# An adaLN layer with routed experts: late blocks every 11 steps, the count a step later, the w2 wait at its first reader

## What is computed

```python
mod = (_silu(L0_c) @ L0_wmod).reshape(L0_c.shape[0], 6, 1, -1)
sa, ca, ga, sb, cb, gb = (mod[:, 0], ..., mod[:, 5])
ga = (2 * (ga >= 0) - 1) * jnp.maximum(jnp.abs(ga), 0.25)   # gb likewise
h = _layernorm(x, axis=-1) * (1 + ca) + sa
x = x + ga * _L0_attn_ref(h, L0_attn_W_qkv, L0_attn_W_o)    # causal, 16 heads of 16
h = _layernorm(x, axis=-1) * (1 + cb) + sb
x = x + gb * _L0_ffn_ref(h, L0_ffn_router_w, L0_ffn_w1, L0_ffn_w2)
```

## Time and profile before

| | us |
|---|---|
| runs | 2679.83, 2695.54, 2696.79 |
| median | 2695.54 |
| profiled execution | 2677.67 (span 2676.0) |
| experts, from 2124 us to the end | 552 |
| TensorE busy, share of the span | 93% |
| VectorE, ScalarE, GpSimd | 80%, 65%, 21% |

### The profile page before, as it was taken

How to read it: one execution, slowest core, us unless ns; L and a number is a source line. 1 busy time by engine, 2 the same in 40 slices (tenths; PEclk the granted TensorE clock), 3 DMA queues, 4 the chain that set the end, 5 groups by cost and what they waited for, 6 DMA issues and landing times. The chain is left out here.

```text
span 2676.0 us, 51675 instructions
## 1 busy us (share of the span) xinstructions
PE 2484.6 (93%) x16164; PEld 1259.0 (47%) x16164; DVE 2138.3 (80%) x5454; ACT 1727.2 (65%) x3555; POOL 563.3 (21%) x496
## 2 busy tenths in 40 slices
PE   7988999999999999999999999999999699989996
PEld 6863333333333333333333333333332288889896
DVE  6989989888888988888888888888882287867775
ACT  4650576677766666666666666666667566657775
POOL 3451000000001011010101101010101145665554
PEclk9996899999999999999999999999999899999998
DMA  5873224525536363544626353554524556766643
GB/s 193 275 249 89 75 92 149 178 105 157 160 107 191 112 181 110 175 142 147 189 97 191 124 167 117 172 161 139 175 102 156 185 139 152 180 174 133 109 104 70
DMA packets 268011, 396.35 MB, mean 148 GB/s; under 512 B 61712, under 2 KB 163344, under 8 KB 267504
## 3 DMA queue, kind: packets, MB, share of 16 engines
q1 hardware_dynamic: 145504, 164.08, 21.2%
q10 hardware_dynamic: 80240, 151.56, 16.0%
q0 software_dynamic: 42016, 77.59, 12.7%
HBM read 141.16 MB, written 253.00 MB: 147 GB/s over the span
## 5 line engine op out<-in xcount | busy, mean ns | idle before, releaser
L1078 ACT ACTIVATE probs<-ps 128x512 f32<-128x512 f32 (+3 forms) x2400 | 1121.7, 538 | 553.4 <-PE ps L1388 329.8
L1100 DVE TENSOR_REDUCE early<-ps 128x1 f32<-128x512 f32 x1536 | 1000.3, 684 | 111.5 <-PE ps L1293 106.2
L1293 PE MATMUL ps<-kh,qs 96*128 96x512 bf16 (+3 forms) x2560 | 881.9, 362 | 75.4 <-DVE early L1100 34.1
L1388 PE MATMUL ps<-qs,kh 99*128 99x512 bf16 (+3 forms) x2560 | 829.3, 351 | 17.4 <-ACT probs L1078 7.1
L1404 PE MATMUL ps<-probs,vs 128*17 128x512 f32 (+3 forms) x5120 | 598.5, 539 | 0.0
L1293 PEld LDWEIGHTS ps<-kh,qs 96*128 96x128 bf16 x2560 | 250.9, 99 | 688.3 <-DVE early L1100 299.4
L1096 DVE CUSTOM_DVE_ANT_0 junk<-ps,causal 128x128 bf16<-128x128 f32 (+3 forms) x1024 | 480.1, 483 | 49.7 <-PE ps L1293 45.8
L1388 PEld LDWEIGHTS ps<-qs,kh 99*128 99x128 bf16 x2560 | 245.5, 98 | 294.1 <-ACT probs L1078 130.9
L1646 POOL DMA_INDIRECT out<-y,to x142 | 240.4, 1693 | 218.0 <-DVE y L1838 80.1
L982 POOL DMA_INDIRECT rows_out<-row,place_a x96 | 93.4, 973 | 692.0 <-DVE place_a L777 604.9
L1392 PE MATMUL ps<-ident_b,causal_b 128*128 128x128 bf16 x1024 | 213.8, 220 | 0.0
(11 more groups left out here) (246 smaller groups left out, 2866.9 us busy)
## 6 DMA issues: line engine op xcount, KB each, us to landing
rows_out<-empty ACTq DMA_DIRECT2D x129, 1056.0 KB, 4.8
contexts<-ctx_out SPq DMA_DIRECT2D x64, 256.0 KB
xg<-rows_out SPq DMA_DIRECT2D x25, 544.0 KB
q_parts<-parts SPq DMA_DIRECT2D x32, 384.0 KB, 3.4
k_parts<-parts SPq DMA_DIRECT2D x32, 384.0 KB, 4.5
qs<-q_parts SPq DMA_DIRECT2D x64, 192.0 KB, 7.5
kh<-k_parts SPq DMA_DIRECT2D x64, 192.0 KB, 9.0
v_ones<-vt SPq DMA_DIRECT2D x16, 544.0 KB, 5.2
```

The source lines that it names most:

```text
L1078: nc.scalar.activation(probs[u % PB][:, h, q0:TB], bank(s % SB)[:, q0:TB], ACT.Exp, scale=SCALE).then_inc(exp_done, 1)
L1100: nc.vector.tensor_reduce(early[:, h, t, k0 // CW:k0 // CW + 1], tile, AX.X, ALU.max).then_inc(max_done, 1)
L1293: nc.tensor.matmul(tile[:, 0:w], qh[a % HR][0:STACK, t * P:(t + 1) * P], kh[a % HR][0:STACK, k0:k0 + w], start=True, stop=True).then_inc(m ...
L1388: mm = nc.tensor.matmul(tile[:, q0:TB], kh[a % HR][:, kt * P:(kt + 1) * P], qh[a % HR][:, j * TB + q0:(j + 1) * TB], start=True, stop=not ...
```

## The change

Three constants and one wait are changed. PITCH goes from 12 to 11, so the blocks begin at steps 1, 12, 23 and 34. L_COUNT and L_PUT go from 18, 19 to 19, 20. What is computed from them moves: LATE_TABLE 58 to 56; SEND_FROM (4, 7, 10, 12) to (4, 7, 10, 11); STORE_AT (7, 10, 13, 16) to (7, 9, 12, 15); FETCH_X_AT (7, 10) to (7, 9); FETCH_AT stays (0, 4, 7, 10). On GpSimd the token numbers of block 3's rows are written behind add(9), not add(10). TensorE's wait for the split of w2 moves from ahead of the loop into step 1, behind up(3) and ahead of down(0).

```diff
-PITCH = 12
+PITCH = 11
 BASE = [1 + PITCH * m for m in range(LATE_BLOCKS)]
...
-L_ROUTE, L_EXP, L_COMPARE, L_ORDER, L_SHARE, L_COUNT, L_PUT = 14, 15, 16, 17, 17, 18, 19
+L_ROUTE, L_EXP, L_COMPARE, L_ORDER, L_SHARE, L_COUNT, L_PUT = 14, 15, 16, 17, 17, 19, 20
...
                 up(0)
                 up(1)
-                pe.wait_ge(w2l_done, SPLITS // 2)
-                pe.wait_ge(w2lp_done, SPLITS - SPLITS // 2)
                 for q in range(NQ):
...
                     if q + 2 < NQ:
                         up(q + 2)
+                    if q == 1:
+                        pe.wait_ge(w2l_done, SPLITS // 2)
+                        pe.wait_ge(w2lp_done, SPLITS - SPLITS // 2)
                     if q:
                         down(q - 1)
```

## The result

The changed kernel takes 2699.5 us (median of 10 runs, 2694.0 to 2707.4), the kernel before 2685.2 us (median of 10 runs, 2679.8 to 2696.8). The ratio is 1.0045, with a 95% interval of 1.0028 to 1.0063: slower by 0.45%, 12 us. Forecast was 11 us faster. The three runs of before that were shown first happened to hold the two highest of the ten (and the lowest), so their median, from which the forecast was counted, lies 10 us above that of all ten; from 2685.2 us the same 11 us lead to 2674.

What follows compares the result with a forecast made beforehand. TensorE was taken to set the experts' pace until the last 21 half tiles' adds, then GpSimd's scatter-adds. Gains of 2.9, 7.9 and 2.7 us less 2.6 gave 11 us off 2695.5: 2684.5 us, range 2663 to 2699.

Steps and rivals of the forecast that it cites:

- the counts: TensorE's four waits ahead of the counts, 8.9 us: running each count a step later wins 7.9 us (bounds 5 and 8.9).
- so no new wait is seen: Count, put and their users move a step; TensorE's down(BASE + 22) already waits for VectorE's next step, so no added wait.
- the sum: Whole change: 13.5 us earlier at step 56, less 2.6 us at the last block's sends, so 11 us less.
- The prediction's own sign of being wrong: Forecast wrong if new hid_lo waits exceed 5 us before step 56, or the gap ahead of tile 15 is absent.
- 2.9: Start of the experts: gain in us from moving the w2 wait, with up(4) held by VectorE's low_rows(1); bounds 2 and 5.8.
- Part 1: The wait for the split w2: down(0) comes 3.4 us earlier, of which 2.9 us is taken as gain.
- The counts and their clock: Ahead of step 56: 7.9 us from count waits, 2.7 us from slow clock behind the second and third (bounds 0 and 2.7).
- hidden: Tile 17's gather lands at T(56) + 33.2, its transposes are due at T(56) + 35.8: covered by 2.6 us.
- The last sends: Block 3's sends ahead of add(12): down(60) waits until T(56) + 26.7 us; the stretch grows by 2.6 us (bounds 0.9 and 5.4).
- the same lengths as now: From 2413 us to the end, the changed kernel's lengths were to match those of the kernel before.
- The prediction's premise: In the last 21 half tiles GpSimd's scatter-adds pace the work, starting on VectorE's gated sums; earlier gains reach the end.
- The slower one: Rival, chance 0.06: late placement delays the last block's sends, add(12), weigh(14) and tile 17's gather; 2700 us at 15 us late.

Runs made afterwards that it cites:

- after_sends4: The changed kernel with blocks 0 and 1 sending four rows' DMAs behind each add instead of three: 2683.5 us, ratio to before 0.9993.
- after_project3: The changed kernel with the first half of a late block's projection at step 3 of the block instead of 2: 2692.0 us, ratio to before 1.0029.
- pitch_only: The kernel before with only PITCH 11, counts and w2 wait at their old places: 2702.1 us, ratio to before 1.0061.
- count_only: The kernel before with only L_COUNT and L_PUT one step later, at pitch 12: 2675.7 us, ratio to before 0.9969.
- w2_only: The kernel before with only the wait for the split w2 moved to its first reader: 2684.6 us, ratio to before 0.9999.
- w2_dve: The kernel before with the w2 wait in step 1 and all w2 low parts made on VectorE: 2674.3 us, ratio to before 0.9966.
- after_sends12: The changed kernel with SEND_FROM[3] back at 12, so add(12) precedes block 3's eight sends: 2696.0 us, ratio to before 1.0042.
- after_two: The changed kernel with blocks 0 and 1 sending four behind each add and block 3's sends behind add(12): 2684.5 us, ratio to before 1.0014.
- after_three: The changed kernel with four sends per add, block 3's sends behind add(12) and the projection's first half a step later: 2668.6 us, ratio to before 0.9948.
- after_four: The kernel of after_three with all low parts of w2 made on VectorE: 2666.2 us, ratio to before 0.9949.
- after_pitch12: The changed kernel with PITCH back at 12: 2673.7 us, ratio to before 0.9954.

## Why the prediction was wrong, point by point

**The step that failed** stands under the counts: "so no new wait is seen", and in the sum, where the pitch itself had no term. I looked for what becomes later or is queued behind something. A shorter pitch makes a late block's parts earlier against everything that isn't tied to the pitch: the adds and sends, which go by tiles. I gave the pitch a row for put and the next transposes and for SyncE's loads, and none for the three other waits between blocks. The prediction's own sign of being wrong, new waits for hid_lo of over 5 us before step 56, came with 15.7 us (4.9, 4.0 and 6.8). The three waits were all in the code that I had read:

- centre(m) waits for the sends of block m - 2. SEND_FROM of blocks 0 and 1 stays 4 and 7, so the last sends stand behind add(6) and add(9), which start in VectorE's steps 31 and 43. Centre came in steps 35 and 47, four behind; it comes in steps 33 and 44, two and one behind. At block 1, four adds, two sends and the landing take about 12 us (2331.25 to 2343.1), three to four steps. This is 14 to 16 us of the loss, shown by after_sends4.
- project(m + 1, 0) waits for turned(m). It moved from the step in which route(m) already waits for the same thing to the step ahead of it: 5.4 us in three waits, gone in after_project3.
- late_transposes(m) waits for modulate(m), a step further on VectorE. At pitch 12 every block falls on the same phase of a tile (BASE is 1 modulo 4); at pitch 11 the phase goes round, onto steps where w1_low or gate_sums can stand ahead of modulate: 6.0 us in three waits. But pitch_only, with the same phases, has 1.3 us of them and count_only, at pitch 12, 3.7. So the larger part comes with the count's new step and not with the phase; that TensorE is then earlier, because it no longer waits for chosen_r, is my reading and no run shows it by itself.

**The w2 wait.** Down(0) came 3.2 us earlier, with 3.4 predicted, and for the reason given. The step from there to "2.9" was wrong: it took the two ups at 1.2 GHz, so that they would fill the pause, and they ran at full clock, so that a gap of 4.9 us was left. In w2_only TensorE's clock behind it was low until about 2160, where before it had risen by 2157. With the granted clock at 0.58 from 2152 to 2160, 2.3 of the 3.2 us were given back by T(16). Part 1 counted a slow clock inside the pause and none behind the new gap. The Trainium skill (SBUF — State Buffer, "Who interferes with whom") has the two engines exclude each other there. The runs agree: in w2_dve, where GpSimd has nothing to do at that place, the 4.44 us become 1.22.

**The counts and their clock.** 7.9 + 2.7 = 10.6 us were predicted ahead of T(56); count_only has 11.3, and 8.7 in the median. Right for the count alone at pitch 12, with 3.7 us of new waits at the transposes, where I had left 1 us, and 2.9 us at tile 17's gather, which I had called hidden: in count_only the placement is a step later. As a term of this change it was too large: at pitch 11 the count's step brings 2.6 to 4 us, since the pitch by itself takes the count waits down to 2.3 us. I took a gain from waits seen at pitch 12 into a kernel at pitch 11. In the changed kernel the gather is hidden, as predicted.

**The last sends.** Mechanism right: eight sends, four adds, two sends; ScalarE and VectorE waiting 6.0 and 6.4 us for the landing; a single gap ahead of tile 15. From T(56) to down(60) I said 26.7 us (bounds 25 to 29.5) and it was 23.4 (2384.55 to 2407.90). Placement was at T(56) + 1.0 and not 2.0, the eight sends took 10.5 us and not 11.5, and the landing 2.4 us behind the last add's issue and not 4.0. GpSimd's rows:

```profile
2385.59 0.96 POOL L1663 DMA_INDIRECT rows_out<-row,place_r  x1 [4.62 <-DVE place_r L777]
...
2394.68 1.40 POOL L1663 DMA_INDIRECT rows_out<-row,place_r  x1 [0.30 <-issue]
2396.38 2.08 POOL L1646 DMA_INDIRECT out<-y,to  x1 [0.30 <-issue]
...
2402.91 1.54 POOL L1646 DMA_INDIRECT out<-y,to  x1 [0.30 <-issue]
```

So this stretch didn't grow (23.4 against 24.1). The mis-sized term was in the safe direction, and undoing it (after_sends12) brought nothing that the ratios show. Part of the 24.1 was chance: w2_only has the same late schedule as the kernel before, its profile has neither ScalarE's pause nor the 4.2 us gap, and its stretch from T(56) to T(68) is 41.5 us against 45.5.

**From T(92) to the end.** I had said "the same lengths as now". In the profiles it was 194.4 us against 189.0. In the kernel before GpSimd's adds had caught up with y in phase 1 and waited for it four times, last at 2508; in the changed kernel they never do so after the sends. There the adds of each tile wait for the landing of those of the tile before, by themselves or through `tails`, whose token numbers ("to") name the row. add(22) is the row at 2496.29 in the kernel before and the one at 2518.51 in the changed kernel:

```profile
2447.00 1.73 POOL L1646 DMA_INDIRECT out<-y,to  x1 [3.96 <-DVE y L1838]
...
2496.29 1.66 POOL L1646 DMA_INDIRECT out<-y,to  x1 [4.73 <-DVE y L1838]
...
2508.12 1.58 POOL L1646 DMA_INDIRECT out<-y,to  x1 [3.39 <-DVE y L1838]
```

```profile
2518.51 2.04 POOL L1646 DMA_INDIRECT out<-y,to  x1 [5.02 <-DVE to L1823]
```

add(22) starts 9.3 us behind T(92) in the kernel before (2496.29 against 2487.02) and 15.0 us in the changed kernel (2518.51 against 2503.47), 5.7 us later; from there to the end both take the same, 179.7 and 179.4 us. So the 5.4 us are the adds' lag, as far as one profile of each can say. The chains that ended last say so too: from 2508 us on in the kernel before, and from 2469 us on in the changed kernel, ahead of its T(92), they run over GpSimd's adds and their landings (but for some 20 us over TensorE in the changed kernel, from 2553 and from 2600 us). The prediction's premise that the adds' start hangs on VectorE's gated sums, so that a gain ahead of them reaches the end, holds in these profiles only where the adds have caught up. The other kernels agree. The five in whose profiles the adds wait for y after the sends (before, w2_dve, after_two, after_three, after_four) have add(22) 9.3 us behind T(92) and 188.0 to 190.8 us from T(92) to the end. The eight in which they don't have 14.8 to 15.7 us and 190.7 to 199.5. In count_only and after_pitch12, 11.5 and 12.9 us are won at T(92) and 1.7 and 2.4 are left at the profile's end, but the medians give 8.7 for both (after_pitch12's profiled execution was the slowest of its twelve, 10 us over their median). How much of a gain the adds swallow in a typical execution can't be settled from one profile each, and why they catch up in some kernels and not in others stays open.

**The rivals.** The slower one had the right sign and the wrong place: it looked for the sends' harm at the last block, where placement comes late. The harm was at the first two, whose sends come late for a buffer. It had 0.06, far too little for a change that moves four blocks against a fixed schedule of sends.

## What to carry to other kernels

When work that is laid out by one count (blocks) is drawn together beside work laid out by another (tiles), write down each wait between the two and its distance in steps before and after; a step gained at the visible wait can cost more at a buffer that loses two or three steps of slack, as it did here. A wait moved to its first reader pays only if nothing else holds that reader, and a gap that is nearly as long in its new place has the slow clock behind it there. Two edits that touch the same wait don't add up: the count's step was worth 8.7 us at one pitch and about 3 at the other. At w2 the edit worth making was to take the other engine off the shared work: 7 us, against nothing for moving the wait.

## What the runs showed of the hardware

- VectorE's tensor_tensor with both inputs in SBUF took 2.69 us (128x512) and 4.44 us (128x1024) beside GpSimd's, and 0.68 and 1.22 us without. Half of w2's low part on GpSimd (two pieces in 7.8 us) cost more than it saved; on VectorE a piece takes 1.7 us.
- What waited for the landing of an accumulating indirect DMA to DRAM (an add) went on 2.0 to 8.0 us behind the end of its last issue: 2.0 in the last half tiles of every kernel, 8.0 once in the kernel before, at 2192. The Trainium skill (DMA: Bandwidth & Descriptors, "Anatomy of one DMA") has about 2 us of fixed cost; the least seen here agrees with it, and most landings took longer.
- In the steps behind T(56) ScalarE pauses for 1.5 to 3.1 us at a time in several kernels, with no semaphore that the profile names behind it ("remote"): in the kernel before, w2_dve, after_sends12, after_two and after_three (and for 8.3 us once, in after_project3). In w2_only, count_only, pitch_only and after_pitch12 it doesn't, and in the changed kernel, where it waits for the adds, it isn't seen. What it is stays open.
